# Interleaving the two groups of a tile on TensorE: both products of cur's high part for both groups, then the low part

## The reference, cut to what matters

```
e  = stack(tbl_f[ids[:, f]])                      # [512, 32 fields, 32 d]
x0 = prev = e
for W in (filter_0, filter_1):                    # [32*32, 128], [32*128, 128]
    z    = einsum('bhd,bmd->bhmd', x0, prev).reshape(b, h*m, d)
    prev = relu(einsum('bpd,pn->bnd', z, W))      # cur
    outs.append(prev)
z = sum over d of concat(outs)                    # [512, 256]
h = relu(concat(z, dense_ctx) @ W_top1 + b_top1)
h = relu(h @ W_top2 + b_top2)
y = h @ W_top3
```

## Time and profile before

| | |
|---|---|
| Median of 3 runs | 882.1 us (880.66 to 882.32) |
| The profiled execution: its own time | 882.07 us |
| Its span, first to last instruction | 880.3 us |
| TensorE (PE) busy | 831.2 us, 94%, 3608 matmuls |
| TensorE weight loads (PEld) busy | 668.5 us, 76%, 3608 |
| VectorE (DVE) busy | 773.2 us, 88% |
| ScalarE (ACT) busy | 725.0 us, 82% |
| GpSimd (POOL) busy | 657.8 us, 75% |
| DMA | 124.38 MB, mean 141 GB/s |

### The profile page before, as it was taken

How to read it: one execution, slowest core, us unless ns; L and a number is a source line. 1 busy time by engine, 2 the same in 40 slices (tenths; PEclk the granted TensorE clock), 3 DMA queues, 4 the chain that set the end, 5 groups by cost and what they waited for, 6 DMA issues and landing times.

```text
span 880.3 us, 17918 instructions
## 1 busy us (share of the span) xinstructions
PE 831.2 (94%) x3608; PEld 668.5 (76%) x3608; DVE 773.2 (88%) x2425; ACT 725.0 (82%) x2425; POOL 657.8 (75%) x642
## 2 busy tenths in 40 slices
PE   0189999999999999999999999999999999999998
PEld 0168888888888888888888878888788888888875
DVE  4158999999999999999999999999999999999995
ACT  2248889988888898988888889888888898888873
POOL 7767898878888888878888878866666766666652
PEclk9999999999999999999999999999999999999999
DMA  7035776667667766676677666766676666766540
GB/s 197 12 88 129 175 167 151 134 137 164 152 149 170 167 149 145 135 155 158 146 165 175 153 145 127 153 158 144 159 172 149 146 128 142 164 144 153 97 92 5
DMA packets 78618, 124.38 MB, mean 141 GB/s; under 512 B 34177, under 2 KB 36993, under 8 KB 78594
## 3 DMA queue, kind: packets, MB, share of 16 engines
q0 software_dynamic: 22240, 68.17, 41.0%
q1 hardware_dynamic: 56354, 55.96, 21.3%
HBM read 54.99 MB, written 3.05 MB: 66 GB/s over the span
## 4 chain that ended last, share of the span: by engine, by line
PE 71%; POOL 16%; DMA 6%; issue 3%; DVE 3%; ACT 0%; DVEq 0%; POOLq 0%
PE bank L864 60%; PE bank L804 9%; DMA parts<-parts 5%; POOL rows L347 4%; POOL pair_low L382 4%; POOL w_sb L366 2%; POOL parts L359 2%; POOL w_sb L373 2%; DVE acc L765 2%; POOL rows L397 2%; POOL half L366 1%; PE bank L870 1%; PE bank L896 1%; PE bank L835 1%; DVE acc L775 0%
## 5 line engine op out<-in xcount | busy, mean ns | idle before, releaser
L545 ACT ACTIVATE parts<-bank,x 128x128 f32<-128x128 f32 x2048 | 588.2, 379 | 97.2 <-PE bank L864 88.7
L765 DVE SCALAR_TENSOR_TENSOR acc<-bank,x,acc 128x128 f32<-128x128 f32 x1792 | 484.4, 342 | 43.8 <-PE bank L864 43.8
L864 PE MATMUL bank<-w_high,cur_high 128*128 128x512 f32 x1024 | 402.3, 393 | 1.6 <-ACT cur_high L492 0.7
L864 PE MATMUL bank<-w_low,cur_high 128*128 128x512 f32 x1024 | 399.3, 390 | 0.0
L864 PE MATMUL bank<-w_high,cur_low 128*128 128x512 f32 x992 | 388.1, 391 | 0.0
L864 PEld LDWEIGHTS bank<-w_high,cur_high 128*128 128x128 f32 x1024 | 192.2, 188 | 49.6 <-DVE acc L765 7.3
L864 PEld LDWEIGHTS bank<-w_low,cur_high 128*128 128x128 f32 x1024 | 192.3, 188 | 40.1
L864 PEld LDWEIGHTS bank<-w_high,cur_low 128*128 128x128 f32 x992 | 186.2, 188 | 40.5
L382 POOL TENSOR_TENSOR pair_low<-pair,pair_high 128x512 fp32r<-128x512 f32 x124 | 158.7, 1299 | 22.1 <-ACT pair_high L481 21.5
L366 POOL TENSOR_TENSOR half<-parts 128x512 f32<-128x512 f32 x64 | 82.8, 1294 | 116.7 <-DMA parts<-parts 116.6
L397 POOL DMA_INDIRECT rows<-table_dram,ids_sb x96 | 97.8, 1019 | 30.8 <-issue 30.3
(11 more groups left out here) (95 smaller groups left out, 555.0 us busy)
## 6 DMA issues: line engine op xcount, KB each, us to landing
parts<-parts POOLq DMA_DIRECT2D x126, 512.0 KB, 6.6
shifts<-x_scratch SPq DMA_DIRECT2D x155, 256.0 KB
x<-x_scratch SPq DMA_DIRECT2D x31, 256.0 KB, 2.9
x_scratch<-turned SPq DMA_DIRECT2D x124, 24.0 KB, 1.8
rows<-table_dram,ids_sb POOLq DMA_INDIRECT x128, 2.5
wt<-w_top_dram SPq DMA_DIRECT2D x2, 512.0 KB, 9.2
w_sb<-w_ab_dram SPq DMA_DIRECT2D x1, 256.0 KB
w_t<-w_ba_dram SPq DMA_DIRECT2D x1, 256.0 KB
```

Source lines behind the costliest of these rows:

```text
L545: ins = nc.scalar.activation(parts[q][ab][:, at:at + N2], act_bank[ab][:, i * N2:(i + 1) * N2], ACT.Copy, scale=x0[u][:, h, 2 * q + ab:2 * ...
L765: nc.vector.scalar_tensor_tensor(out=dst, in0=dve_bank[e % 2 * 2 + ab][:, i * N2:(i + 1) * N2], scalar=x0[u][:, h, 2 * q + ab:2 * q + ab + ...
L864: return nc.tensor.matmul(dst[:], cur_half[u][:, cols], w1_half[:, fields], **flags)
```

## The change

The loop over the four (`ab`, `kind`) of one `e` becomes a loop over `ab`. Within a tile step the six matmuls now go: ScalarE's bank high x high, high x low; VectorE's bank high x high, high x low; ScalarE's bank low x high; VectorE's bank low x high. The wait for ScalarE's bank stays ahead of the first matmul, the wait for VectorE's bank comes ahead of the third (it was the fourth). The special case of slot 0 goes away. Products of the first layer that stood between the two groups (after slots 22 and 24) now stand behind the tile step.

```diff
-                            for ab, kind in ((0, 0), (0, 1), (1, 0), (1, 1)):
-                                g = 2 * e + kind
-                                if kind == 0:
-                                    dst, ready = act_bank[ab], for_act
-
-                                    wait(pe, act_prod, (pair_no * EACH + e - 1) * 2 + ab + 1)
-                                else:
-                                    dst, ready = dve_bank[e % 2 * 2 + ab], for_dve
-
-                                    wait(pe, mac, (pair_no * EACH + e - 1) * (2 * HG))
-                                t = 2 * q + ab
-                                cols, fields = slice(t * P, (t + 1) * P), slice(g * COLS, (g + 1) * COLS)
-                                slot = q * 2 * GROUPS + 4 * e + 2 * ab + kind
+                            for ab in range(2):
+                                t, slot = 2 * q + ab, q * 2 * GROUPS + 4 * e + 2 * ab
+                                cols = slice(t * P, (t + 1) * P)
+                                dst = [act_bank[ab], dve_bank[e % 2 * 2 + ab]]
+
+                                def product(kind, cur_half, w1_half, **flags):
+                                    fields = slice((2 * e + kind) * COLS, (2 * e + kind + 1) * COLS)
+                                    return nc.tensor.matmul(dst[kind][:], cur_half[u][:, cols], w1_half[:, fields], **flags)
+
                                 if slot == 0:
                                     pe.wait_ge(cur_high_ready, c + 1)
-
-                                def product(cur_half, w1_half, **flags):
-                                    return nc.tensor.matmul(dst[:], cur_half[u][:, cols], w1_half[:, fields], **flags)
-
-                                product(cur_high, w1_high, start=True, stop=False)
-                                if slot == 1:
+                                wait(pe, act_prod, (pair_no * EACH + e - 1) * 2 + ab + 1)
+                                product(0, cur_high, w1_high, start=True, stop=False)
+                                product(0, cur_high, w1_low, start=False, stop=False)
+                                wait(pe, mac, (pair_no * EACH + e - 1) * (2 * HG))
+                                product(1, cur_high, w1_high, start=True, stop=False)
+                                product(1, cur_high, w1_low, start=False, stop=False)
+                                if slot == 0:
 
                                     pe.wait_ge(cur_low_ready, c + 1)
-                                    nc.tensor.matmul(act_bank[0][:], cur_low[u][:, 0:P], w1_high[:, 0:COLS],
-                                                     start=False, stop=True).then_inc(for_act, 1)
-                                product(cur_high, w1_low, start=False, stop=False)
-                                if slot > 0:
-                                    product(cur_low, w1_high, start=False, stop=True).then_inc(ready, 1)
-                                if slot in PE_PRODUCT and not (last and u == UNROLL - 1):
-                                    pe_product(pe, c + 1, PE_PRODUCT[slot])
+                                product(0, cur_low, w1_high, start=False, stop=True).then_inc(for_act, 1)
+                                product(1, cur_low, w1_high, start=False, stop=True).then_inc(for_dve, 1)
+                                for at in (slot, slot + 1):
+                                    if at in PE_PRODUCT and not (last and u == UNROLL - 1):
+                                        pe_product(pe, c + 1, PE_PRODUCT[at])
```

## The result

| | before | after |
|---|---|---|
| Median | 882.21 us (4 runs) | 891.67 us (4 runs, 891.15 to 892.45) |
| Ratio, 95% interval | | 1.0108 (1.0093 to 1.0122) |
| Span of the profiled execution | 880.3 us | 890.1 us |

What follows compares the result with a forecast made beforehand. TensorE was taken to lead, with VectorE level in the first half of a chunk. A mean 0.305 us over 31 chunks gave 9.5, less 0.5 for step 0: 882.1 + 9.0 = 891.1 us, range 886 to 899.

Steps and rivals of the forecast that it cites:

- R5: Rival: matmul order does nothing, time within 1 us of 882; chance 0.05 together with other near-cancelling cases.
- R4: Rival: new short stalls halve TensorE's clock once per chunk, costing 53 us in all, 935 us; chance 0.01.
- R3: Rival: faster, 881.1 us, as step 0's waits go and bank waits stay under 0.12 us of cover; chance 0.04.
- the cover of 0.12 us: At TensorE's bank handovers: the first 0.12 us of a weight load's lateness costs nothing.
- (1): VectorE's bank taken one matmul earlier in each tile step: +0.227 us in one kind of chunk, +0.12 in the other.
- (2): ScalarE's bank complete 0.453 us later, pushing VectorE's second instruction of every second chunk by 0.26 us.
- chunk B: The alternate kind of chunk, 24.94 us before, without stalls but with 0.11 us of cover left; forecast +0.38 us.
- (3): ScalarE handing its bank back to TensorE: a 0.14 us stall hidden behind VectorE, booked at nothing, upper bound 4.3 us.
- Chunk A: The kind of chunk, 25.14 us before, where VectorE's late handovers already stall TensorE; forecast +0.227 us.
- R1: Rival: ScalarE's stalls add to VectorE's instead of hiding behind them, 896 to 897 us; chance 0.23.
- R2: Rival: only VectorE's earlier bank counts, ScalarE's push being taken up somewhere, 887 us; chance 0.17.
- (4): Products of steps 0 and 4 moved behind the whole tile step: gain of up to 0.5 us in all.

Runs made afterwards that it cites:

- e4: Kernel before, old matmul order, with VectorE's bank asked for at the third matmul, ScalarE's announced with the fifth, products of steps 0 and 4 behind the tile step: 891.85 us.
- e2: Kernel before, matmul order kept, only the wait for VectorE's bank moved from the fourth to the third matmul of a tile step: 887.21 us, ratio 1.0052.
- e5: Changed kernel with ScalarE's two copies for the transposition behind its second group of a chunk instead of its first: 889.11 us, ratio 1.0086.
- e11: Changed kernel with VectorE's sum of layer 1 (0.60 us) moved from the start of the chunk to its fourth group: 891.11 us, ratio 1.0097.
- e3: Kernel before, old order, ScalarE's bank announced two matmuls later, products of steps 0 and 4 behind the tile step: 888.66 us, ratio 1.0065.
- e1: Kernel before with only the products of steps 0 and 4 moved behind the whole tile step: 881.73 us, ratio 0.9991.
- e8: Changed kernel with an in-between order: VectorE's bank still taken with the third matmul, ScalarE's complete with the fourth instead of the fifth: 887.07 us, ratio 1.0054.
- e10: Kernel before, products of steps 0 and 4 behind the tile step, VectorE's layer-1 sum moved from chunk start to fourth group: 879.63 us, ratio 0.9966.

## Why the prediction was right, and where it wasn't

The forecast of +9.0 us met a measured +9.5 us.

**Right: the cost is handover, not order.** R5 (nothing changes) and R4 (the clock) are out: the clock is 1.00 in the chunks, and 0.91 at the start of both kernels. e4 shows it without the new order. R3 (faster) falls with the waits: VectorE had nothing to spare, and the cover of 0.12 us was used up in both kinds of chunk.

**Right: (1), VectorE's bank.** +0.227 and +0.12 us were booked; e2 shows +0.22 and +0.15, in all 4.8 us (5.1 by the 31 chunks) where 5.4 were booked.

**Right: the push in (2).** 0.26 booked, 0.24 in the trace. e5 takes it away and chunk B falls by 0.08 us on the mean, down to ScalarE's own line. e11 shows it from the other side.

**Wrong in its share: (3), ScalarE's own handback.** "I book it at nothing" held only because VectorE's line, with the push, came out just as long. The bound that I put on it if the cover were gone, 4.3 us, is too small: alone it costs 6.9 us (e3 over e1; 7.9 by the 31 chunks), 0.25 us per chunk. The step that failed is in the working: I took one handback per chunk, with 0.25 us to spare, and priced its stall at 0.14. In the trace after, loads wait for ScalarE at 3.4 places a chunk (107 waits), and the single stall that I had priced costs 0.08 in the chunk shown and 0.07 on the mean. With those at the first and the eighth tile step it makes 0.15 us a chunk. The waits lie at the start and in the first half of the chunk, and there ScalarE had little to spare before the change. Chunk A of the kernel before, up to slot 17 (the columns are those of the earlier trace rows):

```profile
409.49:420.94 11.45, 11.45 (x52) 9.31 (x50) 11.26 (x38) 11.05 (x40) 10.49 (x11) 1.00 0.56 103
```

ScalarE is busy 11.05 of 11.45 us here, 97%, against 82% of the span: it has an extra operation in most groups of this half. What a waiting TensorE sends late, it hands back late again. In e3 TensorE's load at 442.43 waits for ScalarE, and ScalarE's group at 442.51 has stood idle for 0.13 us and starts 0.04 after the matmul that completed its bank; the same happens at 445.3 and 448.1.

So R1, whose reason was this line, was nearer on the mechanism than its 23% said, though its addition was wrong: by the 31 chunks e2 and e3 make 13.0 us apart and 10.5 together. In a chunk A VectorE's line is the longer (25.36 in e2, 25.39 after). In a chunk B the two are level: VectorE's with the push comes to 24.94 + 0.38 = 25.32, ScalarE's alone to 25.30 (e3, the window of B), measured 25.35. That the forecast was close owes something to luck: these two lines happen to be of one length. R2 (only the order term, 887) described e8 and e2, not the change.

**Right within its size: (4).** e1 gives 0.7 us by the medians and 0.5 by the 31 chunks, the forecast 0.5, and the medians can't tell either from nothing. The 131 ns per matmul of the Trainium skill ("TensorE: Matmul & The Clock Gate", section "Back-to-back issue gap") has no support in any run; the page's 216 ns stays 5% under the 0.2267 us of this stream.

## What to carry to other kernels

When an order of matmuls is changed, draw for each bank two times, when it is asked for and when it is complete, and compare each shift with what that bank had to spare at its tightest place in the loop, at every place and not at one. An engine that is busy 82% of the time, as ScalarE was before, can be busy 97% in the half where its extra work lies. Where two engines read banks, their lines overlap rather than add, so relieving only one of them may win nothing (e11), while the same relief pays where the other has room (e10). And before moving a step off a full engine, look for a DMA that starts from it.

## What the runs showed of the hardware that was not expected

Matmuls that aren't held up still have two paces. In e10 the first 50 distances of a chunk are 0.2267 us each, on the mean of 27 chunks. From the first product of layer 1 to eleven matmuls before the chunk's end they are 0.2315 us on the mean, with hardly a load late. Three matmuls of a product in the timeline of e10,

```profile
419.14 0.39 PE L804 MATMUL bank<-pair_high,w_high 128*128 128x512 f32 x1
419.37 0.40 PE L804 MATMUL bank<-pair_high,w_low 128*128 128x512 f32 x1
419.61 0.39 PE L804 MATMUL bank<-pair_low,w_high 128*128 128x512 f32 x1
```

are 0.23 and 0.24 apart. The same slower pace follows each stall for some ten matmuls. In the kernel after, such distances (all under 0.24 us, taken together) make up 0.15 of the 0.32 us that a chunk has gained. The sum of the forecast has no term for them; it goes by when the handovers come. In e10 it is 48 x 0.0048 = 0.23 us per chunk, 7 us in all, the largest thing left that these traces show. What causes it was not tried.
